# A one-batch first piece per expert, one weight transfer per expert and thirteen weight buffers in a two-layer attention and expert kernel

## The reference, cut

```python
scores = jax.nn.softmax(x @ classifier_weight.T, axis=-1)
_, topk_idx = jax.lax.top_k(scores + e_score_correction_bias[None, :], 6)
w_full = jnp.zeros((T, 40)).at[jnp.arange(T)[:, None], topk_idx].add(topk_w)
def body(out, xs):
    Wgu, Wd, we = xs
    gate, up = jnp.split(x @ Wgu.T, 2, axis=-1)
    y = jax.nn.silu(gate) * up @ Wd.T
    return (out + we[:, None] * y, None)
```

## Time and profile before

| | |
|---|---|
| three runs | 1060.6, 1060.65, 1065.75 us |
| median | 1060.65 us |
| the profiled execution: its own time | 1065.29 us |
| its span, first to last instruction | 1063.7 us |
| granted TensorE clock, mean | 0.95 |
| PE, PEld, DVE, ACT busy | 88%, 68%, 66%, 39% of the span |
| experts' stage | from about 385 us to 612 us of the span |

### The profile page before, as it was taken

One profiled execution on the slowest core, in us unless ns is written; L12 is line 12 of the kernel. 1 busy time (PEld: TensorE's weight loads), 2 busy tenths in 40 slices (PEclk: granted clock), 3 DMA queues, 4 the chain that ended last, 5 costly groups with the idle time before them and its releaser, 6 DMA issues.

```text
span 1063.7 us, 20769 instructions
## 1 busy us (share of the span) xinstructions
PE 932.7 (88%) x7430; PEld 724.7 (68%) x7430; DVE 697.2 (66%) x1518; ACT 414.1 (39%) x970; POOL 136.6 (13%) x129
## 2 busy tenths in 40 slices
PE   2996999999979779999998856899999987898987
PEld 1663778788857459899988745577777765455554
DVE  4454677777735715455554464788888874999995
ACT  1441566666655441111111122466565654111211
POOL 7021000000011430000000004000000001344442
PEclk9997999999986999999999978899999988999999
DMA  9688454454042630202121305554444200000000
GB/s 284 198 235 192 85 101 91 95 88 88 17 132 62 200 130 16 78 16 62 35 61 60 109 26 129 112 91 88 88 87 88 60 2 1 5 12 10 13 13 18
DMA packets 103231, 87.07 MB, mean 82 GB/s; under 512 B 44002, under 2 KB 94562, under 8 KB 103010
## 3 DMA queue, kind: packets, MB, share of 16 engines
q1 hardware_dynamic: 103122, 85.58, 33.3%
HBM read 67.52 MB, written 17.79 MB: 80 GB/s over the span
## 4 chain that ended last, share of the span: by engine, by line
issue 32%; PE 28%; DVE 27%; DMA 7%; SPq 2%; POOL 2%; ACT 1%; POOLq 0%; DVEq 0%; ACTq 0%
PE ps L794 12%; DVE ext L1219 8%; PE ps L801 7%; DMA qscr<-qsp 3%; DVE Pr L1167 2%; DVE Pr L1172 2%; DVE Pr L1170 2%; DMA Qz<-mT 2%; PE ps L651 2%; PE ps L561 2%; DMA wgu<-wgu 1%; DVE amh L1399 1%; DVE Pr L1421 1%; POOL ksp L492 1%; PE ps L700 1%
## 5 line engine op out<-in xcount | busy, mean ns | idle before, releaser
L1219 DVE TENSOR_REDUCE ext<-ps 112x2 f32<-112x750 f32 x256 | 235.5, 933 | 56.8 <-PE ps L623 54.3
L986 ACT ACTIVATE Pr<-ps 125x448 f32<-125x448 f32 x384 | 199.0, 542 | 101.9 <-PE ps L637 88.7
L794 PE MATMUL ps<-xT,wgu 128*128 128x224 f32 x704 | 150.1, 356 | 12.5 <-issue 4.9
L794 PEld LDWEIGHTS ps<-xT,wgu 128*128 128x128 f32 x704 | 132.9, 191 | 23.1 <-issue 12.4
L637 PE MATMUL ps<-Qz,Kp 98*125 98x224 f16 x768 | 132.8, 269 | 15.8 <-DMA Qz<-mT 13.7
L623 PE MATMUL ps<-Kp,Qz 96*112 96x375 f16 x512 | 123.8, 334 | 11.8 <-DMA Qz<-qscr 10.6
L637 PEld LDWEIGHTS ps<-Qz,Kp 98*125 98x125 f16 x768 | 96.4, 140 | 49.9 <-DMA Qz<-mT 18.6
L691 PE MATMUL ps<-wv,ctx 128*125 128x256 f32 x384 | 121.9, 402 | 0.8 <-ACT Vx L992 0.7
L561 PE MATMUL ps<-ctx,wk 128*128 128x375 f32 x256 | 95.1, 519 | 25.0 <-DMA bqk<-bqk 14.2
L1337 DVE TENSOR_TENSOR Pr<-Pr,ps 128x224 f32<-128x224 f32 x88 | 34.1, 388 | 125.5 <-ACT Pr L1057 68.2
L873 PE MATMUL ps<-Pr 128*112 128x352 f32 x256 | 85.5, 480 | 16.9 <-DVE Pr L1421 16.5
(11 more groups left out here) (139 smaller groups left out, 1094.9 us busy)
## 6 DMA issues: line engine op xcount, KB each, us to landing
ctx<-ctxT SPq DMA_DIRECT2D x64, 375.0 KB, 3.7
Kp<-kscr SPq DMA_DIRECT2D x96, 187.5 KB, 4.1
kscr<-ksp SPq DMA_DIRECT2D x32, 375.0 KB, 3.8
wgu<-wgu SPq DMA_DIRECT2D x32, 256.0 KB, 2.8
Qz<-qscr SPq DMA_DIRECT2D x192, 28.0 KB, 3.9
wdn<-wdn SPq DMA_DIRECT2D x32, 128.0 KB, 3.0
qscr<-qsp SPq DMA_DIRECT2D x32, 112.0 KB, 3.3
X<-x_in SPq DMA_DIRECT2D x1, 1792.0 KB, 11.7
```

The lines of the kernel that those rows point to most:

```text
L794: last = mm(ps[:, bank, half_ * CT:(half_ + 1) * CT], wgu_sb[e % NE][:, q, EI * half_:EI * half_ + EI], xT2[:, q, c * CT:(c + 1) * CT], st ...
L986: A(Pr[g % 2][0:KC, j, GI * t:GI * t + GI, :].rearrange("r h q -> r (h q)"), ps[0:KC, 4 + k % 2, 0:GI * S], ACT.Exp, scale=scale).then_inc ...
L1219: V.tensor_reduce(ext[0:S, 2 * p:2 * p + 2], ps[0:S, 2 * (p % 2):2 * (p % 2) + 2, 0:M], AX_X, red).then_inc(row_maximum_taken, 1)
```

## The change

The pieces of an expert become one of one batch (batch 0), seven of two batches (1 to 14) and one of one batch (15), nine in all. The mask now covers batches 1 to 15. A product of a piece of one batch is 112 columns wide, its down part is one product. The two weight arrays become one in HBM, `wexp`, with 3 KB per partition and expert, and one transfer of 384 KB per expert. There are 13 weight buffers: 4 of their own, 2 in `Pr[1]` and 7 in `Pr[0]`. SP loads experts 0 to 3 where it did, 4 and 5 once the first attention's values are summed, 6 to 12 behind the last key store and the router's end, and expert e from 13 on when the first piece's gate and up products of expert e - 11 are done.

```diff
-CH = 8
-CB = B // CH
-CT = CB * S
+PIECES = [(0, 1)] + [(b, min(2, B - b)) for b in range(1, B, 2)]
+CH = len(PIECES)
+CT = 2 * S
-NE = 4
+NE, NO, NP = 13, 4, 2
+EW = 2 * C2 * EI + D
...
+        own_expert = [sb(f"expert{p}", [128, EW]) for p in range(NO)]
...
+        at = 8 * CT + 2 * C2 * M
+        expert_sb = [t[:, :] for t in own_expert] + [spare1[:, at + EW * n:at + EW * (n + 1)] for n in range(NP)]
+        expert_sb += [spare[:, EW * n:EW * (n + 1)] for n in range(NE - NO - NP)]
...
                     def load_expert(e):
-                        sp.dma_start(wgu_sb[e % NE][:, :, :], wgu[e].rearrange("(c p) o -> p c o", p=128)).then_inc(
-                            gate_up_weights_loaded[e % NE], 16)
-                        sp.dma_start(wdn_sb[e % NE][:, :], wdn[e]).then_inc(down_weights_loaded[e % NE], 16)
-
-                    for e in range(NE):
+                        sp.dma_start(expert_sb[e % NE], wexp[e]).then_inc(expert_loaded[e % NE], 16)
+
+                    for e in range(NO):
                         load_expert(e)
...
                     load_ctx(2, 0)
+                    sp.wait_ge(values_summed, B)
+                    for e in range(NO, NO + NP):
+                        load_expert(e)
...
+                    sp.wait_ge(tokens_routed, 1)
+                    for e in range(NO + NP, NE):
+                        load_expert(e)
                     for e in range(NE, ER):
                         sp.wait_ge(first_gate_up_ready, e - NE + 3)
                         load_expert(e)
...
+                        b, nb = PIECES[c]
                         for half_ in (0, 1):
                             for q in range(C2):
-                                last = mm(ps[:, bank, half_ * CT:(half_ + 1) * CT],
-                                          wgu_sb[e % NE][:, q, EI * half_:EI * half_ + EI],
-                                          xT2[:, q, c * CT:(c + 1) * CT], start=(q == 0), stop=(q == C2 - 1))
+                                last = mm(ps[:, bank, half_ * CT:half_ * CT + nb * S],
+                                          expert_sb[e % NE][:, EI * (2 * q + half_):EI * (2 * q + half_ + 1)],
+                                          xT2[:, q, b * S:(b + nb) * S], start=(q == 0), stop=(q == C2 - 1))
...
-                        for v in range(CB):
-                            last = mm(ps[0:S, bank, v * D:(v + 1) * D], h[:, v * S:(v + 1) * S], wdn_sb[e % NE][:, :],
+                        for v in range(PIECES[c][1]):
+                            last = mm(ps[0:S, bank, v * D:(v + 1) * D], h[:, v * S:(v + 1) * S], expert_sb[e % NE][:, C2 * 2 * EI:],
                                       start=True, stop=True)
...
-                        pe.wait_ge(down_weights_loaded[e % NE], 16 * (e // NE + 1))
...
-                    ch.link(V.tensor_reduce(used[0:S, :], W[0:S, CB * ET:].rearrange("q (b e) -> q e b", e=ET)[:, 0:ER, :],
+                    ch.link(V.tensor_reduce(used[0:S, :], W[0:S, ET:].rearrange("q (b e) -> q e b", e=ET)[:, 0:ER, :],
```

More of the change, by code:

```diff
@@ L94, in step, with build @@
         self.eng.reg_add(self.reg, self.reg, n)
-def build(nc, x, ctxT, attn, wc, ebias, powers, wgu, wdn, fg, fu, fd, out):
+def build(nc, x, ctxT, attn, wc, ebias, powers, wexp, fg, fu, fd, out):
     ctx = ExitStack()
@@ L149, in build @@
         top, rsum, above, zw, zb = (sb(n, [128, B]) for n in ("top", "rsum", "above", "zw", "zb"))
-        wgu_sb = [sb(f"wgu{p}", [128, C2, 2 * EI]) for p in range(NE)]
-        wdn_sb = [sb(f"wdn{p}", [128, D]) for p in range(NE)]
+        own_expert = [sb(f"expert{p}", [128, EW]) for p in range(NO)]
         pow_sb = sb("pow_sb", [1, ER // 2])
@@ L175, in build @@
         hT = spare1[:, 3 * FI + D + C2 * S:3 * FI + D + (C2 + 6) * S].rearrange("p (c q) -> p c q", c=6)
-        kfull = [spare1[:, CH * CT + C2 * M * n:CH * CT + C2 * M * (n + 1)].rearrange("p (c m) -> p c m", c=C2)
+        kfull = [spare1[:, 8 * CT + C2 * M * n:8 * CT + C2 * M * (n + 1)].rearrange("p (c m) -> p c m", c=C2)
                  for n in (0, 1)]
+        at = 8 * CT + 2 * C2 * M
+        expert_sb = [t[:, :] for t in own_expert] + [spare1[:, at + EW * n:at + EW * (n + 1)] for n in range(NP)]
+        expert_sb += [spare[:, EW * n:EW * (n + 1)] for n in range(NE - NO - NP)]
         at = 3 * FI + D + (C2 + 6) * S
@@ L241, in build @@
         router_exps_ready = sem("router_exps_ready")
-        gate_up_weights_loaded = [sem(f"gate_up_weights_loaded{p}") for p in range(NE)]
-        down_weights_loaded = [sem(f"down_weights_loaded{p}") for p in range(NE)]
+        expert_loaded = [sem(f"expert_loaded{p}") for p in range(NE)]
         used_by_token = sem("used_by_token")
@@ L790, in gate_up, with down @@
                     def gate_up(e, c, bank, done):
+                        b, nb = PIECES[c]
                         for half_ in (0, 1):
                             for q in range(C2):
-                                last = mm(ps[:, bank, half_ * CT:(half_ + 1) * CT],
-                                          wgu_sb[e % NE][:, q, EI * half_:EI * half_ + EI],
-                                          xT2[:, q, c * CT:(c + 1) * CT], start=(q == 0), stop=(q == C2 - 1))
+                                last = mm(ps[:, bank, half_ * CT:half_ * CT + nb * S],
+                                          expert_sb[e % NE][:, EI * (2 * q + half_):EI * (2 * q + half_ + 1)],
+                                          xT2[:, q, b * S:(b + nb) * S], start=(q == 0), stop=(q == C2 - 1))
                         last.then_inc(done, 1)
-                    def down(e, h, bank, done):
-                        for v in range(CB):
-                            last = mm(ps[0:S, bank, v * D:(v + 1) * D], h[:, v * S:(v + 1) * S], wdn_sb[e % NE][:, :],
+                    def down(e, c, h, bank, done):
+                        for v in range(PIECES[c][1]):
+                            last = mm(ps[0:S, bank, v * D:(v + 1) * D], h[:, v * S:(v + 1) * S], expert_sb[e % NE][:, C2 * 2 * EI:],
                                       start=True, stop=True)
@@ L807, in first_gate_up @@
                         if e < ER:
-                            pe.wait_ge(gate_up_weights_loaded[e % NE], 16 * (e // NE + 1))
+                            pe.wait_ge(expert_loaded[e % NE], 16 * (e // NE + 1))
                             if e >= 2:
@@ L818, in first_down @@
                             pe.wait_ge(first_added, e - 1)
-                        down(e, hfirst[e % 2], 4 + e % 2, first_down_ready)
+                        down(e, 0, hfirst[e % 2], 4 + e % 2, first_down_ready)
                     def rest_gate_up(e, c):
@@ L829, in rest_down @@
                         pe.wait_ge(rest_added, n)
-                        down(e, hrest[c % 2], 6 + c % 2, rest_down_ready)
+                        down(e, c, hrest[c % 2], 6 + c % 2, rest_down_ready)
                     first_gate_up(0)
@@ L1056, in first_silu @@
                             act.wait_ge(first_gate_up_ready, e + 1)
-                            A(hfirst[e % 2], ps[:, e % 2, 0:CT], ACT.Silu).then_inc(first_silu_ready, 1)
+                            A(hfirst[e % 2][:, 0:S], ps[:, e % 2, 0:S], ACT.Silu).then_inc(first_silu_ready, 1)
                     def rest_silu(c):
@@ L1061, in rest_silu @@
                         act.wait_ge(rest_gate_up_ready, rest_n.now())
-                        A(hrest[c % 2], ps[:, 2 + c % 2, 0:CT], ACT.Silu).then_inc(rest_silu_ready, 1)
+                        n = PIECES[c][1] * S
+                        A(hrest[c % 2][:, 0:n], ps[:, 2 + c % 2, 0:n], ACT.Silu).then_inc(rest_silu_ready, 1)
                     first_silu(0)
@@ L1334, in _, with gate @@
                     rest_gates, rest_adds = Tally(dve, "dve_rest_gates"), Tally(dve, "dve_rest_adds")
-                    def gate(h, bank, done):
-                        V.tensor_tensor(h, h, ps[:, bank, CT:2 * CT], ALU.mult).then_inc(done, 1)
+                    def gate(c, h, bank, done):
+                        h = h[:, 0:PIECES[c][1] * S]
+                        V.tensor_tensor(h, h, ps[:, bank, CT:CT + PIECES[c][1] * S], ALU.mult).then_inc(done, 1)
                     def add(e, c, bank, done):
-                        for v in range(CB):
-                            b = CB * c + v
+                        for v in range(PIECES[c][1]):
+                            b = PIECES[c][0] + v
                             xb = X[:, b * D:(b + 1) * D]
@@ L1349, in first_gate @@
                             dve.wait_ge(first_silu_ready, e + 1)
-                            gate(hfirst[e % 2], e % 2, first_gated)
+                            gate(0, hfirst[e % 2], e % 2, first_gated)
                     def first_add(e):
@@ L1360, in rest_gate @@
                         dve.wait_ge(rest_silu_ready, rest_gates.now())
-                        gate(hrest[c % 2], 2 + c % 2, rest_gated)
+                        gate(c, hrest[c % 2], 2 + c % 2, rest_gated)
                     def rest_add(e, c):
```

(7 more changed lines are left out.)

## The result

The changed kernel took **1080.47 us** (median of four runs, 1074.78 to 1081.64), the kernel before 1062.12 us (median of four: the three runs above and one more beside the changed kernel; 1060.6 to 1065.75). The ratio is 1.016, 95% interval 1.011 to 1.020, so it is slower. The forecast was 1080, slower by 1.8%. The profiled execution took 1081.26 us, its span is 1079.4.

What follows compares the result with a forecast made beforehand. PE bounds the experts' stage, its jumps stalling on code blocks. Products with mask -2.4, stall +19.9, ends -0.5, clock +2.6 give +19.6 us on 1060.65: 1080 us, 8 in 10 for 1067 to 1089.

Steps and rivals of the forecast that it cites:

- Bound: Experts' stage: PE's products fill most of it; 13.4 us are stalls of jumps waiting for code, weights not guilty.
- the first rival: Unused experts' jumps: code is there in time, all stalls go, -16.3 us, 1044 us; chance 4%.
- Mask: Batch 1 joins the mask, so expert 10 with 3 tokens there becomes a used one, costing 18.0 us.
- the third rival: The mask does not grow, rounding leaves expert 10 out: -18.0 and +3.7 us, 1066 us; chance 5%.
- Products: PE's expert pieces: one batch costs 1.39 us, two cost 2.375; with expert 10 the sum is 206.6 us, 2.4 less.
- Blocks: Stretches of unused experts: 3, 5 and 8 code blocks at 3.6 us each; stall 33.3 us, +19.9 against before.
- the formula in the prediction: Stall of a stretch: 3.6 us less one piece's time per further expert, less queued work (1.1 us before, 0.7 after).
- my second rival: Weight transfers make code blocks late: blocks at 2.5 us make it even, at 2.4 us 1058 us; chance 6%.
- Clock: Experts 7 and 22 start at 1.2 GHz after sparse stretches: +2.6 us for both, bounds 0 and 6.8.
- Ends: End of the experts' stage: one add of 0.44 us instead of two after the last down product, -0.5 us.
- The sign and the size of 14 to 27 us: Kernel slower (84%); the experts' stage of 227 us grows by 14 to 27 us, otherwise the prediction is wrong.

Runs made afterwards that it cites:

- the loop in the kernel before: The kernel before with PE's pieces 2 to 7 of the rest written as a loop, same products in the same order: 1047.28 us, ratio 0.984.
- Weights alone: The changed kernel's thirteen weight buffers and single transfers per expert, with the pieces and mask of the kernel before: 1062.8 us, ratio 0.998.
- The loop with the thirteen buffers: Old pieces and mask, thirteen buffers and one transfer per expert, plus PE's rest pieces as a loop, against the kernel before: 1047.93 us, ratio 0.988.

## Why the prediction was right

*Bound.* That jumps wait for code blocks, and that weights only tie with them, was the step that carried the sign. Buffers alone leave the time as it was (ratio 0.998), less code takes the whole stall away, dead code brings 55 us. Shown, not only argued.

The page cited with the first rival (the Trainium skill, Runtime: NRT & Kernel Launch, section Instruction fetch mechanics) has a second rule that fits instead: a taken branch to a target outside a window of two blocks has to fetch it first. The trace agrees: one jump of a stretch is short, the next is not.

*Mask.* 18.0 us of products for expert 10, 14.3 net of jumps in the third rival and 13 with the clock in the expectation: the run with the old mask gives 11.

*Products.* 1.39 us for a one-batch piece was too much: 1.31 in the trace, so the pieces cost 63 x 2.375 + 41 x 1.31 = 203.3 us, 5.7 less than before instead of 2.4. The price came from the query projections, where eight pairs took 0.97 to 1.12 us with the last one's tail. Here the down products start 0.88 us after gate and up, and not the 0.96 of 8 x 0.12.

*Blocks.* Their number, 3, 5 and 8, was right; their time of 3.6 us was too high, 3.33 measured (53.3 us for 16). The fit of the formula in the prediction took each stretch's own block time (3.8, 3.5 and 3.6 us); with 3.6 throughout it gives 2.6, 5.0 and 5.1 us for the three stretches, where 3.1, 4.5 and 4.5 were seen, so it is good to half a microsecond per stretch. The stall by the same formula is 16 x (3.33 - 1.31) - 2.1 = 30.2 us instead of 33.3, and the difference to before 16.8 instead of 19.9. Intervals in these kernels go from 3.2 to 3.8, the longer ones mostly while weights are in flight. That transfers delay blocks was my second rival. No run isolates it; in the changed kernel a block takes 3.31 us in the last stretch, with the DMA engines at 0.03, and 3.31 and 3.38 in the others, at 0.44 and 0.43. So nothing here comes near the 2.5 us from which it would have decided.

*Clock.* Taken at 2.6 us, measured 2.5 + 2.7 = 5.2 for experts 7 and 22 (21.07 and 21.26 against 18.56). Not in the sum at all: expert 1 takes 20.63 us, and before it took 18.7 between the same two branches (391.9 to 410.5), so 2.0 more. The clock is 0.50 from 390 to 396, against 0.72 in the earlier trace rows. It fell at 390 in both kernels, but here PE had stood idle for the block that failed to come at 389.4, and the lower level lasted longer. That the idle time is the reason is likely and not shown: no run changes it alone.

*Ends.* The start was taken at 0. From the first SiLU (389.6) to the first product of expert 1's rest (393.5) it is 3.9 us, 0.8 more than before; most of the 2.73 us for that block lies in it.

Together: from the first to the last SiLU 631.0 - 389.6 = 241.4 us against 610.1 - 390.6 = 219.5 before, 21.9 more. The terms give -5.7 + 16.8 + 5.2 + 2.0 + 0.8 = 19.1; 2.8 us are not assigned. Two terms too dear and two too cheap or missing met at nearly the right sum, so the closeness of 1080 to 1080.47 is in part luck. The sign and the size of 14 to 27 us are not.

**The 5 us that come back.** The spans differ by 15.7 us only, not 21.9. The first SiLU comes 1.0 us earlier, and the second attention runs level until its last batch (from the last SiLU to the last row maximum 255.3 us in both). Windows (columns as in the earlier trace rows) over the last 18 us of the second attention, first of the kernel before, then of the changed one:

```profile
866.00:884.00 18.00, 14.55 (x188) 10.89 (x187) 6.74 (x21) 7.99 (x17) 0.00 (x0) 0.72 0.01 2
```

```profile
884.00:902.00 18.00, 14.91 (x251) 10.54 (x249) 10.39 (x29) 10.76 (x24) 0.00 (x0) 1.00 0.01 2
```

Before, the clock was 0.72 here, after it was 1.00. From the last row maximum to the last exponential it took 882.4 - 865.4 = 17.0 us before and 898.3 - 886.3 = 12.0 after. Of the other nine traces seven took 11.9 to 12.0 us for it, among them the loop in the kernel before, and two took 15.8 and 15.7 (*Weights alone* and *The loop with the thirteen buffers*). All three long ones are among the five kernels with the old pieces; the six with the new pieces show none. So these 5 us come and go among kernels with the old pieces, and with one trace of each it stays open whether the change has a part in them. They may also be why the profiled execution of before stood 4.6 us over its median, which the prediction had noted without a cause; that isn't shown, since only one execution of that kernel was traced. By the medians the change is 18.4 us.

## What to carry to other kernels

Count the instructions between a jump and its target, in blocks of code, before shortening the work that covers it: here every further unused expert of a stretch cost a block's 3.3 us though its products took 1.31, and making them narrower mostly laid the wait bare. A loop on one engine, with the same products in the same order, gave 1.6% where thirteen buffers and fewer transfers gave nothing that could be told from noise. And where a change moves the border of what data decides (here one batch into a mask), work out from the inputs what falls on the other side.

## What the runs showed of the hardware

- A block of 256 instructions reaches PE 3.2 to 3.8 us after the one before it when jumps run ahead (means of a stretch), and blocks that are jumped over are loaded as well (62 blocks for 32 x 1.95). Where a jump led 1.95 blocks on, it took 5.1 us.
- The border can stall straight code too, with no branch in the gap: 2.73 us in the middle of a gate-and-up group.
- A chain of waits named the weight transfers for 6.8% of the stage; with thirteen buffers that wait was gone, and the ratio of the times was 0.998. A tie is shown by taking one of the two away, not by the chain.
- In the stretch of six of the changed kernel, with one-batch pieces and code waits between them, PE was busy for 10.86 of 16.88 us at a granted clock of 0.75, a mean of the two levels (1.2 and 2.4 GHz), and the used expert that began at the lower one took 2.7 us more. With first products issued twice it was busy there for 14.90 of 23.30 us, and the clock stayed at 1.00.
